# An edge-count loop on VectorE: order of additions and comparisons, place of a wait, load of a register

## What is computed

```python
edge_index = jnp.stack([src, dst])
x = _layernorm(x + _L0_gnn_ref(x, edge_index, W, b, diffusion_weights))  # diffusion, 3 steps
x = _layernorm(x + _L1_gnn_ref(x, W, b, src, dst, 1024))                 # sum of messages
x = _layernorm(x + _L2_gnn_ref(x, wc, wn, bias, edge_index))             # mean of messages
x = _layernorm(x + _L3_gnn_ref(x, edge_index, Ws, Wb, a_w, a_b))         # 8 attention heads
```

## Time and profile before

| what | value |
|---|---|
| median of 3 runs | 399.75 us (398.93, 399.75, 400.77) |
| span of the profiled execution | 398.2 us |
| the median less that span | 1.55 us |
| TensorE busy | 370.9 us (93%) |
| VectorE busy | 281.4 us (71%), 596 instructions |
| ScalarE busy | 238.5 us (60%) |
| GpSimd busy | 103.3 us (26%) |
| line 1254, 64 additions | 23.1 us, mean 361 ns |
| line 1235, 64 comparisons | 22.3 us, mean 389 ns |

### The profile page before, as it was taken

How to read it: one execution, slowest core, us unless ns; L and a number is a source line. 1 busy time by engine, 2 the same in 40 slices (tenths; PEclk the granted TensorE clock), 3 DMA queues, 4 the chain that set the end, 5 groups by cost and what they waited for, 6 DMA issues and landing times.

```text
span 398.2 us, 7856 instructions
## 1 busy us (share of the span) xinstructions
PE 370.9 (93%) x2704; PEld 217.5 (55%) x2704; DVE 281.4 (71%) x596; ACT 238.5 (60%) x414; POOL 103.3 (26%) x95
## 2 busy tenths in 40 slices
PE   1799989999999999999999999999899999999990
PEld 0254337554444444444444444444457889999990
DVE  7768998855996677024675444555596888999984
ACT  9879975667831255322464111366875999999444
POOL 4620000009950056600486000067400000112110
PEclk9999998999999999999999999999999999999996
DMA  5950004104200000000144000033302022310005
GB/s 180 391 184 2 1 0 144 71 0 123 91 0 2 0 0 3 2 0 0 27 95 92 0 0 3 0 70 75 68 2 105 9 84 73 103 60 2 5 3 213
DMA packets 27448, 22.71 MB, mean 57 GB/s; under 512 B 19537, under 2 KB 19729, under 8 KB 27409
## 3 DMA queue, kind: packets, MB, share of 16 engines
q1 hardware_dynamic: 26544, 19.06, 15.9%
q10 hardware_dynamic: 864, 3.15, 2.4%
HBM read 15.87 MB, written 2.13 MB: 45 GB/s over the span
## 4 chain that ended last, share of the span: by engine, by line
PE 82%; DVE 8%; ACT 4%; issue 2%; DVEq 1%; DMA 1%; POOL 0%; ACTq 0%
PE ps L742 19%; PE ps L1101 14%; PE ps L1042 7%; PE ps L951 7%; PE ps L992 7%; PE ps L905 7%; PE ps L914 7%; PE ps L775 4%; PE ps L895 3%; DVE c L1254 3%; PE ps L884 3%; PE ps L796 2%; DVE adj L1235 1%; ACT c L461 1%; ACT cts L486 1%
## 5 line engine op out<-in xcount | busy, mean ns | idle before, releaser
L742 PE MATMUL ps<-big,xTs 128*128 128x512 f16 x384 | 84.3, 379 | 0.5 <-DMA xTs<-big 0.5
L742 PEld LDWEIGHTS ps<-big,xTs 128*128 (+1 forms) x384 | 37.0, 98 | 44.0 <-issue 0.6
L651 ACT ACTIVATE big<-big,uvt 128x1024 bf16<-128x1024 f32 x55 | 58.7, 1145 | 0.0
L555 ACT ACTIVATE big<-xcur,nmr,rstd (+1 forms) x24 | 19.5, 813 | 34.9 <-DVE nmr L1360 34.9
L775 PE MATMUL ps<-big,xTs 128*128 128x512 f32 x64 | 35.6, 653 | 0.0
L427 POOL TENSOR_TENSOR big<-xcur,big x16 | 18.5, 1155 | 62.2 <-ACT xcur L556 61.5
L461 ACT ACTIVATE big<-ps 128x512 f16<-128x512 f32 (+2 forms) x17 | 9.7, 572 | 39.7 <-PE ps L742 30.0
L397 POOL TENSOR_TENSOR big<-xTs,big 128x2048 f16<-128x2048 f32 x4 | 16.2, 4083 | 58.9 <-ACT big L461 58.9
L444 POOL TENSOR_TENSOR xcur<-xcur,c 128x512 f32<-128x512 f32 x6 | 7.1, 1184 | 89.5 <-DVE c L1563 89.5
L1042 PE MATMUL ps<-big,cst 128*128 128x260 f16 x256 | 29.8, 275 | 0.0
L1254 DVE TENSOR_TENSOR c<-c,ps 128x80 f32 (+31 forms) x64 | 23.1, 361 | 9.4 <-PE ps L796 6.2
(11 more groups left out here) (210 smaller groups left out, 691.4 us busy)
## 6 DMA issues: line engine op xcount, KB each, us to landing
big<-u_rows ACTq DMA_DIRECT2D x6, 512.0 KB, 3.7
xTs<-in_xT SPq DMA_DIRECT2D x2, 1024.0 KB, 9.4
xcur<-in_x SPq DMA_DIRECT2D x1, 2048.0 KB, 17.6
out<-xcur SPq DMA_DIRECT2D x8, 256.0 KB, 2.6
big<-in_W SPq DMA_DIRECT2D x1, 1024.0 KB, 6.0
cts<-in_W3T SPq DMA_DIRECT2D x1, 1024.0 KB, 13.0
xTs<-in_W1T SPq DMA_DIRECT2D x1, 1024.0 KB, 5.3
xTs<-in_wc SPq DMA_DIRECT2D x1, 1024.0 KB, 8.1
```

What stands on the lines that cost most here:

```text
L651: act.activation(above[:, a % AHEAD, :], uf[:, h % 2], ACT.Relu, scale=BIG, bias=vb[:, j, h:h + 1]).then_inc(S["above_in"], 1)
L742: return mm(bank, lhs(k)[a], rhs(k)[b], start=start and k == 0 and n == 0, stop=stop and k == KT - 1 and n == 2)
```

## The change

The comparisons of a quad are made one at a time, and the second one comes behind the second addition. The wait for the product is attached to the addition instead of standing ahead of it as an instruction. The column load has no bounds any more, and it is called at the end of a quad, for the next quad.

```diff
-            def key_hots(q):
+            def key_hots(q, w):
                 n = NT * window(q)
-                if q >= RING:
+                if w == 0 and q >= RING:
                     dve.wait_ge(S["win_done"], 2 * (q - RING) + 2)
-                for w in range(2):
-                    tt(hot_key[...], iota_rep[:, 0:n, 0:NC], spread(key16[:], q, n)[...], ALU.is_equal).then_inc(S["key_hot"], 1)
+                tt(hot_key[...], iota_rep[:, 0:n, 0:NC], spread(key16[:], q, n)[...], ALU.is_equal).then_inc(S["key_hot"], 1)
...
             def first_columns(g):
-                v = dve.value_load(packed[0:1, g:g + 1], min_val=0, max_val=2 ** 30 - 1)
+                v = dve.value_load(packed[0:1, g:g + 1])
                 return [(v if c == 0 else v >> 10 * c) & 1023 for c in range(3)]
 
             def add_window(w, first):
                 m = window(w // 2)
-                dve.wait_ge(S["win_done"], w + 1)
                 if w:
                     dve.wait_ge(S["win_free"], w)
                 cells = c32[:, :, bass.ds(first.with_bounds(min_val=0, max_val=N - m), m)]
-                tt(cells, cells, ps[...].rearrange("p (a w) -> p a w", w=m),
-                   ALU.add).then_inc(S["win_free"], 1)
+                added = tt(cells, cells, ps[...].rearrange("p (a w) -> p a w", w=m), ALU.add)
+                added._wait_ge(S["win_done"], w + 1)
+                added.then_inc(S["win_free"], 1)
...
-            first = []
+            first = first_columns(0)
             for q in range(NQ):
-                if 2 * q == len(first) or 2 * q + 1 == len(first):
-                    first += first_columns(len(first) // 3)
                 add_window(2 * q, first[2 * q])
                 if q + LOOK < NQ:
-                    key_hots(q + LOOK)
+                    key_hots(q + LOOK, 0)
                 add_window(2 * q + 1, first[2 * q + 1])
+                if q + LOOK < NQ:
+                    key_hots(q + LOOK, 1)
                 if q + LOOK < NQ and not lo_by_act(q + LOOK):
                     lo_hots(q + LOOK)
                 elif tiles_low < NT and h_quad(tiles_low) + (4 if q < NQ - 2 else 3) <= q:
...
+                if len(first) < 2 * q + 4 and len(first) < NG:
+                    first += first_columns(len(first) // 3)
```

More of the change, by code:

```diff
@@ L1228, in _ @@
             dve.wait_ge(S["key_in"], 1)
-            def key_hots(q):
+            def key_hots(q, w):
                 n = NT * window(q)
-                if q >= RING:
+                if w == 0 and q >= RING:
                     dve.wait_ge(S["win_done"], 2 * (q - RING) + 2)
-                for w in range(2):
-                    tt(hot_key[:, q % RING, w * NC * n:(w + 1) * NC * n].rearrange("p (k c) -> p k c", c=NC), iota_rep[:, 0:n, 0:NC],
-                       spread(key16[:], q, n)[:, :, w * NC:(w + 1) * NC], ALU.is_equal).then_inc(S["key_hot"], 1)
+                tt(hot_key[:, q % RING, w * NC * n:(w + 1) * NC * n].rearrange("p (k c) -> p k c", c=NC), iota_rep[:, 0:n, 0:NC],
+                   spread(key16[:], q, n)[:, :, w * NC:(w + 1) * NC], ALU.is_equal).then_inc(S["key_hot"], 1)
             def lo_hots(q):
@@ L1253, in add_window @@
                 cells = c32[:, :, bass.ds(first.with_bounds(min_val=0, max_val=N - m), m)]
-                tt(cells, cells, ps[:, WINDOW_BANKS[w % 4], 0:NT * m].rearrange("p (a w) -> p a w", w=m),
-                   ALU.add).then_inc(S["win_free"], 1)
+                added = tt(cells, cells, ps[:, WINDOW_BANKS[w % 4], 0:NT * m].rearrange("p (a w) -> p a w", w=m), ALU.add)
+                added._wait_ge(S["win_done"], w + 1)
+                added.then_inc(S["win_free"], 1)
             def h_lower(t):
@@ L1259, in h_lower @@
                 tt(cur[:, 0, 1, t, :], ps[:, h_bank(t), :], cur[:, 0, 0, t, :], ALU.subtract).then_inc(S["h_lo"], 1)
-            key_hots(0)
+            key_hots(0, 0)
+            key_hots(0, 1)
             dve.wait_ge(S["nslo_in"], 1)
             lo_hots(0)
-            key_hots(1)
+            key_hots(1, 0)
+            key_hots(1, 1)
             lo_hots(1)
-            key_hots(2)
+            key_hots(2, 0)
+            key_hots(2, 1)
             dve.wait_ge(S["c32z"], 2)
```

## The result

The changed kernel takes 394.12 us (median of four runs, 392.94 to 394.51), the kernel before 399.85 on the same chip (four, 398.93 to 400.77). The ratio is 0.985, with an interval of 0.983 to 0.987, so the change saves 5.7 us. The profiled execution has a span of 392.0 us against 398.2: 6.2 less. The forecast had 3.3.

What follows compares the result with a forecast made beforehand. From about 27 us the loop was taken to run at VectorE's (DVE's) pace. Gains of 0.65 (quads 8 to 11), 2.15 (turns) and 0.5 (wait) made 3.3 us: 396.45, say 396.5 us, range 395.4 to 399.2.

Steps and rivals of the forecast that it cites:

- the turnaround: From the end of one VectorE addition to the next start: 0.265 us without a column shift, 0.345 with one.
- Step 1, turns: Quads 12 to 28: one comparison after each addition nearly covers the time to the next; gain 2.15 us.
- seven bare quads: Quads of 12 to 28 with no third VectorE work after additions and comparisons; gain 0.30 each, 2.1 us.
- Step 2, the load: Column load between quads: dropping its check gains nothing extra; bounds nothing, and 2.7 us lost if it showed everywhere.
- Step 3, the wait: Product's wait at the addition: a semaphore instruction may vanish between additions; 0 to 1.1 us, 0.5 taken.
- Step 4, quads 8 to 11: VectorE's stretch from 24.72 to 31.32 us gets shorter, so quad 12 starts 0.65 us earlier.
- Before quad 8 PE bounds, and I take nothing: Loop ahead of quad 8: TensorE (PE) sets the pace there, so no gain was counted.
- Quads 29 to 31 … stay as they are: Last three quads, without comparisons: no gain of their own, so the casts start 3.3 us earlier.
- PE and ScalarE: Rival: PE, ACT (ScalarE) or the load takes most of the gain, leaving 0.85 us, 398.9; chance 0.17.
- the slower side: Rival: the attached wait lengthens the time between additions to 0.50 us; +2.5 us, 402.25; chance 0.05.
- The clock's low stretch: Rival: the 0.50 clock of 68 to 70 us falls on 16 adjacency products, costing 3.6 us; 400.05; chance 0.06.
- The first transpose: Sign behind the loop: PE's first transpose starts at about 64.5 us instead of 67.86 if the prediction is right.

Runs made afterwards that it cites:

- a_sep: Changed kernel with the product's wait as an instruction of its own ahead of the addition again; 396.73 us, ratio 0.993 to the kernel before.
- b_turns: Kernel before with only the comparisons one at a time, the second behind the second addition; separate waits and checked load stay; 399.37 us, ratio 0.998.
- a_bounds: Changed kernel with the bounds of the column load again; 395.87 us, ratio 0.989 to the kernel before, two executions only.
- b_wait: Kernel before with only the product's wait attached to the addition; 396.13 us, ratio 0.991.
- h_early: The change in quads 0 to 7 only, the form of the kernel before from quad 8 on; 398.61 us, ratio 0.995.
- b_warm2: Kernel before with extra products filling TensorE's pauses ahead of quads 0, 2, 3, 4 and between windows of quads 3 to 5; 398.69 us, ratio 0.996.
- a_swap: Changed kernel with an addition's waits exchanged: product's wait ahead, wait for the own previous addition attached; 391.20 us, ratio 0.981 to the kernel before.

## Why the prediction was half right

**What bounds the loop: right.** From quad 12 on DVE set the pace, and its idle of 2.57 was the turnaround. It fell to 0.06, and PE's waits with it.

**Step 1, turns: right, with a condition.** Forecast 2.15. `a_sep` is that step with the unchecked load and without the attached wait: 30.48 less 28.53 is 1.95. By kind of quad, as periods of VectorE, it gave 1.98 in the seven bare quads, 0.43 in the six with low one-hots and -0.47 in the four with a lower half, beside 2.1, 0.4 and -0.35 forecast; the whole change gave 2.40, 0.44 and -0.11. The condition is the short load: with the check left in (`b_turns`) the same turns gave nothing. One reading was wrong, without harm to the sum: low one-hots did not cover the turnaround before.

**Step 2, the load: right, the bound too wide.** The load is nearly hidden, and with its check it shows by about 0.2 in a bare quad, as in `b_turns`. But not at every load: 1.04 in quads 12 to 28, and 0.55 in quads 8 to 11 (`a_bounds`), not 2.7. Low one-hots and lower halves cover it.

**Step 3, the wait: right mechanism, middle too low.** The instruction left the path: 0.07 at each turnaround, 0.79 in quads 12 to 28 against the 0.5 taken. In the whole kernel the same wait is worth 3.2 to 3.4 by the ratios of `a_sep` and `b_wait`, more than its share of the loop from quad 8 on; the part ahead of quad 8 in it (1.70 in `b_wait`, nothing in `a_sep`) is open to chance.

**Step 4, quads 8 to 11: 0.92 against 0.65.**

**"Before quad 8 PE bounds, and I take nothing": this step failed**, and it holds 2.08 of the 2.9 us by which the spans beat the forecast. PE was indeed the engine that was last there, but its start depended on VectorE. Ahead of its first pair it had waited for additions at 13.46, 14.09 and 14.70 (0.39, 0.30, 0.26); after, only twice (0.39, 0.19), and its second and third pair start 0.81 earlier. By that quad 8 moves by 0.81, as TensorE has no recorded wait from its first pair to quad 8. The remaining 1.3 are TensorE's rate, full from 19.64 instead of 23.33. In the terms of the trace I took busy for bound: I never put the same matmul of two times beside each other, 2.07 at 18.10 and 1.06 at 24.17. The experiments bear both halves out (`h_early` 1.5 us, `b_warm2` 1.5 with VectorE unchanged). How the gain divides in a given run is not settled, because the rate's onset moves by 1.7 us between executions of the kernel after and by 2.5 with the form of before.

**"Quads 29 to 31 … stay as they are": 0.22 missed.** They too have bare turnarounds, three of them, 0.07 each. I had counted the saving for 17 first and 7 second gaps and stopped at quad 28.

The account: 3.3 forecast, 2.08 ahead of quad 8, 0.27 in quads 8 to 11, 0.09 in 12 to 28, 0.22 to the cast, 0.24 behind it: 6.2.

**The rivals.** PE and ScalarE took nothing from this change: one new wait of 0.3. They do take it from `a_swap`. The turnaround shrank, so the slower side is out. The clock's low stretch is absent in the three profiles of the kernel after and cost 0.7 in `h_early`. The first transpose, forecast at about 64.5, came at 61.90.

## What to carry to other kernels

An engine that is busy all through a stretch may be slow there, or started late: compare the duration of one shape early and late in the trace before you call the stretch bound and its waits free. When a wait in front of an instruction also stands in front of its address arithmetic, attach to the instruction the wait that ends last, and let the other one stand ahead. A serial path of short instructions is sped up by what is put between its steps, but only if the sequencer's work (a load and its checks) fits beside one of them; parts of such a change can be worth nothing alone.

## What the runs showed of the hardware that I had not expected

- TensorE's rate at the start of the execution is half the later one (2.05 us and 1.07 for the same pair of 128x512 f32 matmuls). It ended at 23.33 before, 19.64, 19.45 and 17.97 in three executions of the kernel after, 17.12 in `b_warm2`. The granted clock in the profile's rows reads 1.00 all the while, but the trace has no record of the clock before these times.
- Two waits ahead of one instruction cost a semaphore instruction of 21 ns and some 50 ns to the next register operation; with one ahead and one attached there is none (63 to 0).
- With the address worked out ahead and the wait for the own previous addition attached, additions followed one another after 0.03 us (0.98 for two of 0.48), where it was 0.28.
